# Row sums of the probabilities in two pieces of 256 columns for each half of the keys, in every other group

## What is computed

```python
xn = rms_norm(x, gamma)
qkv = xn @ w_qkv
qkv = qkv.reshape(b, n, 3, HEADS, DIM_HEAD)
qkv = jnp.transpose(qkv, (2, 0, 3, 1, 4))
q, k, v = (qkv[0], qkv[1], qkv[2])
q = q * scale
sim = jnp.einsum('bhid,bhjd->bhij', q, k)
attn = jax.nn.softmax(sim, axis=-1)
out = jnp.einsum('bhij,bhjd->bhid', attn, v)
out = jnp.transpose(out, (0, 2, 1, 3)).reshape(b, n, DIM_INNER)
return out @ w_out
```

## Time and profile before

| | us |
|---|---|
| median of 3 runs | 2074.19 |
| lowest and highest | 2070.89, 2075.51 |
| the profiled execution | 2072.37 |
| its span, first to last instruction | 2070.6 |
| TensorE busy | 1981.0 |
| VectorE busy | 1730.3 |
| GpSimd busy | 1566.5 |
| ScalarE busy | 1463.1 |

### The profile page before, as it was taken

How to read it: one execution, slowest core, us unless ns; L and a number is a source line. 1 busy time by engine, 2 the same in 40 slices (tenths; PEclk the granted TensorE clock), 3 DMA queues, 4 the chain that set the end, 5 groups by cost and what they waited for, 6 DMA issues and landing times.

```text
span 2070.6 us, 25597 instructions
## 1 busy us (share of the span) xinstructions
PE 1981.0 (96%) x8290; PEld 1410.7 (68%) x8290; DVE 1730.3 (84%) x1964; ACT 1463.1 (71%) x1804; POOL 1566.5 (76%) x783
## 2 busy tenths in 40 slices
PE   7999999998799999999999999999999999999987
PEld 5777767785467667766766776676667667666655
DVE  5777787665869998998999899899989989999855
ACT  4555455445278887887888788778878877887864
POOL 4332233225178998999899999989989998999993
PEclk9999999998989999999999999999999999999998
DMA  7211102210502130312213031221303122131000
GB/s 189 52 32 42 36 12 35 53 31 17 125 0 60 35 72 14 77 32 55 60 36 72 14 77 31 57 57 38 72 14 77 28 60 48 44 72 16 13 16 21
DMA packets 80679, 97.85 MB, mean 47 GB/s; under 512 B 33275, under 2 KB 36779, under 8 KB 80167
## 3 DMA queue, kind: packets, MB, share of 16 engines
q1 hardware_dynamic: 80550, 96.22, 21.1%
HBM read 44.25 MB, written 1.44 MB: 22 GB/s over the span
## 4 chain that ended last, share of the span: by engine, by line
PE 66%; ACT 2%; DVE 1%; issue 1%; POOL 1%; DMA 0%; SPq 0%; POOLq 0%; ACTq 0%
PE ps L989 12%; PE ps L967 11%; PE ps L990 11%; PE ps L1004 11%; PE ps L1007 11%; PE ps L1016 3%; PE ps L1023 3%; ACT p_h L1385 1%; PE ps L949 1%; PE ps L950 1%; PE ps L951 1%; PE ps L749 1%; PE ps L748 1%; PE ps L747 1%; PE ps L975 0%
## 5 line engine op out<-in xcount | busy, mean ns | idle before, releaser
L662 POOL TENSOR_TENSOR p_l<-p_raw,p_h 128x1024 fp32r<-128x1024 f32 x512 | 1240.7, 2452 | 103.9 <-ACT p_h L1385 95.9
L1752 DVE TENSOR_REDUCE m_part<-ps 128x1 f32<-128x1024 f32 x512 | 621.0, 1216 | 125.9 <-PE ps L967 125.9
L1382 ACT ACTIVATE p_raw<-ps 128x1024 f32<-128x1024 f32 x512 | 567.5, 1108 | 212.6 <-PE ps L990 212.5
L1385 ACT ACTIVATE p_h<-ps 128x1024 fp32r<-128x1024 f32 x512 | 524.0, 1023 | 0.0
L989 PE MATMUL ps<-qa,ka 128*128 128x512 f32 x1024 | 444.2, 434 | 1.7 <-issue 1.6
L1004 PE MATMUL ps<-p_h,v_hl 128*128 128x512 f32 x1024 | 404.6, 395 | 7.6 <-POOL p_l L662 7.5
L990 PE MATMUL ps<-qb,kb 65*128 65x512 f32 x1024 | 409.4, 400 | 0.0
L1746 DVE TENSOR_REDUCE l_sum<-p_raw 128x128 f32<-128x1280 f32 x256 | 377.0, 1476 | 13.5 <-ACT p_raw L1382 13.5
L967 PE MATMUL ps<-ka,qa 128*128 128x512 f32 x1024 | 336.3, 410 | 7.2 <-DVE m_part L1752 6.6
L1007 PE MATMUL ps<-p_l,v_hl 128*64 128x512 f32 x1024 | 321.6, 395 | 0.0
L1734 DVE TENSOR_REDUCE p_raw<-p_raw 128x128 f32<-128x1024 f32 x256 | 308.6, 1208 | 9.5 <-ACT p_raw L1382 9.5
(11 more groups left out here) (200 smaller groups left out, 2297.2 us busy)
## 6 DMA issues: line engine op xcount, KB each, us to landing
g_bc<-g_scratch SPq DMA_DIRECT2D x64, 256.0 KB, 5.1
xn<-r_scratch SPq DMA_DIRECT2D x63, 256.0 KB, 4.0
qa<-qk_hi SPq DMA_DIRECT2D x112, 128.0 KB, 2.4
ka<-qk_hi SPq DMA_DIRECT2D x56, 128.0 KB, 2.4
kb<-qk_hi SPq DMA_DIRECT2D x56, 128.0 KB, 2.4
ka<-xn SPq DMA_DIRECT2D x28, 128.0 KB, 2.3
qb<-xn SPq DMA_DIRECT2D x28, 128.0 KB, 2.3
ka<-qk_low SPq DMA_DIRECT2D x28, 128.0 KB, 2.4
```

The lines of the kernel that those rows point to most:

```text
L662: nc.gpsimd.tensor_tensor(p_l[:, g % 4, :, :], slots(g), p_h[:, g % 4, :, :].bitcast(fp32), ALU.subtract).then_inc(pl_done, 1)
L1382: af(slots(g), s_t, ACT.Exp).then_inc(raw_done, 1)
L1385: af(p_h[:, g % 4, :, :], s_t, ACT.Exp).then_inc(ph_done, 1)
L1752: nc.vector.tensor_reduce(m_part[:, it, half:half + 1], ps[:, first_bank:first_bank + 2, :].rearrange("p b n -> p (b n)"), AX.X, ALU.max). ...
```

## The change

The row sums are made in two pieces of 256 columns for each half and not in four of 128. The pieces of the whole sum stand in groups 0 and 2, those of the first half in groups 4 and 6; groups 1, 3, 5 and 7 have none. Inside a group the order stays: the piece, the small things, the maximum.

```diff
--- before.py
+++ after.py
@@ -49,7 +49,7 @@
 SCALE_GROUP = 3
 COPY_GROUP = 2
 ACC = GROUPS // 2
-PIECES = 4
+PIECES = 2
 PIECE = CH // PIECES
 MOVES_HI, MOVES_LO = 4, 2
 
@@ -1786,10 +1786,10 @@
                 last = isinstance(head, int) and head == HEADS - 1
                 summed = before(head, c, 1)
                 for g in range(GROUPS):
-                    if g >= GROUPS // 2:
-                        first_half_sum(head, c, g - GROUPS // 2)
-                    elif exists(summed[0]):
-                        whole_sum(*summed, g)
+                    if g >= GROUPS // 2 and g % 2 == 0:
+                        first_half_sum(head, c, (g - GROUPS // 2) // 2)
+                    elif g < GROUPS // 2 and g % 2 == 0 and exists(summed[0]):
+                        whole_sum(*summed, g // 2)
                     if c == 0 and g in LATE_LOW and late_project:
                         low_qk(head + 1, 1 - par, LATE_LOW[g], spare_bank(NC - 1), qk_hi, qk_low[LATE_LOW[g] % 2], True)
                     if (c, g) in LOW_QK and project:
```

## The result

| | before | after |
|---|---|---|
| median, us | 2073.31 (4 runs) | 2211.62 (4 runs) |
| lowest and highest | 2070.89, 2075.51 | 2208.24, 2213.69 |
| span of the profiled execution | 2070.6 | 2208.4 |
| VectorE busy | 1730.3 | 1724.2 |
| TensorE's mean granted clock | 0.982 | 0.987 |

The changed kernel takes 1.067 times as long (95% interval 1.065 to 1.070), 138 us more. The forecast was 2199 us, in a range of 2170 to 2235.

What follows compares the result with a forecast made beforehand. TensorE was taken as the bound, held up by late VectorE maxima: +133 us in 60 chunks, +0.6 in the first, -8.7 for value-weight waits, +125 in all, forecast 2199 us, range 2170 to 2235.

Steps and rivals of the forecast that it cites:

- The bound, and the place of the loss: Attention: TensorE sets the pace, late maxima go straight into the span; pairs 1 and 3 lose 0.94 and 1.03 us.
- the chunk walked: The traced attention chunk, recomputed with the longer VectorE slots: pair 4 at 1245.04, not 1243.06; first half 1.98 us longer.
- The direction in spite of less work: Whole kernel: 6% slower although VectorE has 14 us less work; slower by over 0.2% given chance 0.94.
- The 14 us forecast for its slots: VectorE's sum pieces and maxima: 9.86 us a chunk where it had 10.08, 14 us less over 64 chunks.
- The returned wait on the value weights: Even heads' chunk 1, group 3: TensorE's 8.7 us of waits for GpSimd's low part of the value weights go.
- The sum: Whole kernel: +133 us from 60 chunks, +0.6 from the first chunk, -8.7 for the value weights, so +125 us.
- the walk: Step-by-step timing of pairs, pieces and maxima in each kind of chunk: 17.7 us lost per eight chunks, 133 over 60.
- the surcharge of 0.10 us: TensorE's score pairs: the step behind a pair that had to wait is about 0.10 us longer.
- Faster by fixed parts: Rival: VectorE's sum is the bound, so less work shortens the kernel to 2056 to 2066 us; chance 0.04.
- One loss in a chunk: Rival: VectorE's lead at the chunk's start hides the loss at pair 1; 2137 us; chance 0.06.
- The clock falls as well: Rival: TensorE, less steadily busy in the attention, gets a clock of 0.97; about 2240 us; chance 0.12.

Runs made afterwards that it cites:

- The kernel with the early value weights: Against the kernel before: GpSimd makes the low part of the value weights one group earlier, behind group 0 of chunk 1; 2057.8 us, ratio 0.993.
- The kernel with one piece: Against the changed kernel: each sum in one piece of 512 columns, in group 0 and in group 4; 2568.8 us, ratio 1.242.
- the changed kernel with the short maximum: Against the changed kernel: maximum over 512 of the 1024 scores, scores sixteen times smaller, output not the reference's; 2068.1 us, ratio 0.997.
- five and three pieces: Against the kernel before: whole sums in five pieces in groups 0 to 4, first-half sums in three in groups 5 to 7; 2071.0 us, ratio 0.999.
- the kernel before with the short maximum: Against the kernel before: maximum over 512 of the 1024 scores, scores sixteen times smaller, output not the reference's; 2062.2 us, ratio 0.995.

## Why the prediction was right, and what it missed

**The bound, and the place of the loss: right.** TensorE waits for the maxima at pairs 1 and 3, in every chunk in which whole sums stand ahead of maxima. The first half of the chunk walked was to be 1.98 us longer; it is 2.07 (11.60 against 9.53). From pair 0 to the next pair 0 the losses are 2.2 in odd heads' chunk 1 (forecast 1.98), 2.7 in their chunk 2 (2.48) and 2.7 in their chunk 0 (2.48). The size of the waits was less well told. The forecast took the 48 us of the weight loads up to 130 to 180; on the weight loads they are 202.4, above that range, and on TensorE's own stream, which is what the span feels, they went from 6.6 to 127.2. That stream before:

```profile
PE ps L967 <- DVE m_part L1752: 6.6, 15, 0.8
```

**The direction in spite of less work: right.** VectorE's sum of busy time fell by 6 us, and nothing of that came back. The 14 us forecast for its slots are not refuted by the 6: the last 0.08 us of an instruction counts as busy on its own only where VectorE then idles, and it now waits for a pair 261 times and not 139, some 10 us by this estimate.

**The returned wait on the value weights: right.** None of the 8.7 us is left.

**The sum: 13 us too small**, 125 for a measured 138. Over eight chunks in the middle the loss is 19.3 us where the forecast had 17.7 less 1.1 for the returned wait, so 16.6. Two terms of the walk that were too small make the difference.

First, the surcharge of 0.10 us behind a waiting pair was put on the next step alone. It also stands between that pair and its own maximum: 1300.74 to 1301.50 is 0.76, and not the 0.66 of a pair that did not wait. In the walk this lengthens the way from pair 1 to pair 3 in all eight chunks, and that from pair 3 to pair 5 in three: 11 x 0.10 = 1.1 us.

Second, for chunk 3 the forecast set TensorE's projection or output between a long piece and its pair against the low part, and took no account of who else waits for these low parts. The next thing on TensorE in the same spare bank waits for them, not for a maximum. The kernel after, all engines, where the low part stands behind a first-half piece:

```profile
1259.40 0.63 PE L967 MATMUL ps<-ka,qa 128*128 128x512 f32 x2
...
1260.38 0.74 DVE L1724 SCALAR_TENSOR_TENSOR xn<-ps,qk_scale,qk_hi 128x512 fp32r<-128x512 f32 x1
...
1261.22 1.02 PE L1016 MATMUL ps<-l_sum,inv_c 128*1 128x512 f32 x2 [0.27 <-issue]
...
1263.21 0.63 PE L967 MATMUL ps<-ka,qa 128*128 128x512 f32 x2
```

The low part would have been done at about 1260.0 behind a short piece; it ends at 1261.12, and the column sums start at 1261.22, where TensorE stood for 0.27. The step from pair 4 to pair 5 is 3.81 and not 3.47. The output product two groups later does the same (3.67 for 3.18). These are 0.34 + 0.49 in each chunk 3, 1.7 us in eight chunks. With the first term it makes 2.8, which accounts for the 2.7 by which 19.3 is above 16.6. The experiments bear on it: with the long first-half pieces alone this wait is longer (0.76 at one of the column sums), and with the pieces in the odd groups, where no low part stands behind one, it is gone. The rows of the kernel with long first-half pieces:

```profile
PE ps L1017 <- issue: 10.5, 14, 0.8
...
PE ps L1024 <- issue: 3.6, 14, 0.3
```

These are the waits of TensorE's own stream ahead of the column sums and the output product in the kernel with long first-half pieces, 14 of each, one for each chunk 3 with low parts; in the kernel with the odd groups there are no such rows. The trace calls them issue, since VectorE's low part had just ended when they did. Late low parts were in the expectation for the long first-half pieces, 2108 with them and 2097 without; 2106 was measured. In the kernel with long whole sums alone, pairs 1 and 3 wait as in the changed one, but the two steps in chunk 3 are 3.48 and 3.19 again, as before the change, and the chunk loses 2.2 us and not 3.0.

**Too large in turn.** 19.3 us in eight chunks would make 145 over 60, and 138 were measured. Most of the difference stands at two of the seven places of the value weights. The sum took the wait there as gone, but not the slow clock behind it. Chunk 1 of the first head came out 3.1 us shorter than before the change, where an even head's chunk 1 is usually 0.8 longer; at the place of 1512 us it is 0.7 shorter. These are 5.4 us together. The stretch from 550 to 640 us, before and after:

```profile
550.00:640.00 90.00, 79.67 (x307) 52.74 (x306) 70.16 (x63) 53.56 (x62) 59.85 (x27) 0.91 0.13 29
```

```profile
550.00:640.00 90.00, 76.25 (x314) 49.99 (x313) 71.24 (x55) 53.52 (x62) 59.91 (x27) 0.98 0.13 31
```

In the kernel before, the clock was granted at 0.91 there, in the kernel after at 0.98. The kernel with the early value weights bears this out: it takes only these waits away, and it too gains more at these two places (5.4 and 2.9 us) than at the other five. That the forecast of 2199 is only 13 us off owes a little to this: without the clock it would have been further off.

**The rivals.** "Faster by fixed parts" fell with the sign; that two kinds of piece of similar length cost 110 and 34 us shows why: the sum of VectorE's work says nothing here. "One loss in a chunk" fell: both pairs wait. "The clock falls as well" did not come: the attention ran at 1.00. The kernel with one piece, with gaps of 3.4 us and not of 1, shows it.

## What to carry to other kernels

Where two engines hand work to each other through a single buffer, what counts is the longest stretch of other work ahead of the handed-over step, not the busy share: pieces should be cut so that piece and step together fit in the partner's own time between two steps, and the room in the next step cannot be saved up. Merging instructions to save their fixed part (0.06 us here) is worth it only where nobody waits behind them, or where the partner has enough other work to cover the longer piece, as in most of groups 4 to 7; here it saved some 15 us of work and cost 138. And each thing that stands behind a piece has its own waiting partner: follow every one of them, not only the one with the largest wait.

## What was not expected of the hardware

- TensorE's clock was at 1.00 up to the wait ahead of the short projection matmuls of the value weights and went to 1.2 GHz right behind it, in some places and not in others. With the first wait of each trace left out (2.04 or 2.05 us, with a slow stretch behind it in all four), this came behind one of six waits of 1.09 to 1.16 us (the kernel before), two of six of 1.32 to 1.36 (the changed kernel with the short maximum), four of six of 1.52 to 1.56 (five and three pieces) and all six of 1.54 to 1.57 (the kernel before with the short maximum). Longer waits had it more often, but the last two show that the length alone does not settle it. Each is one execution.
- Behind a weight load that had to wait, a pair of matmuls lasts 0.72 to 0.73 us and not 0.63. This one delay of 0.10 us shows twice: the next matmul comes later, and so does the engine that reads the result (0.76 us from pair to maximum where 0.66 is usual).
